# Dense expert layer of a four-layer model: rounding the weights to their high halves moves from GpSimd to ScalarE

## The reference

```python
def _L1_ffn_ref(hidden_states, Wg, Wu, Wd):      # Wg, Wu: 8 x 256 x 1024, Wd: 8 x 1024 x 256
    x = hidden_states.reshape(-1, H)
    def expert_step(acc, w):
        wg, wu, wd = w
        h = jax.nn.silu(x @ wg) * (x @ wu)
        return (acc + h @ wd, None)
    acc, _ = jax.lax.scan(expert_step, jnp.zeros_like(x), (Wg, Wu, Wd))
    return acc.reshape(B, S, H)
x = x + jnp.tanh(g_ffn[1]) * _L1_ffn_ref(_layernorm(x, axis=-1), ...)
```

## Time and profile before

| what | value |
|---|---|
| median of 3 runs | 2197.32 us (2195.87 to 2203.53) |
| profiled execution, its own time | 2206.47 us |
| its span, first to last instruction | 2204.7 us |
| mean granted TensorE clock | 0.924 |
| TensorE matmul busy | 1898.4 us (86%) |
| VectorE busy | 1589.9 us (72%) |
| ScalarE busy | 1046.2 us (47%) |
| GpSimd busy | 793.9 us (36%) |
| the dense stage | from about 516 us to 1574 us of the span |

### The profile page before, as it was taken

One profiled execution on the slowest core, in us unless ns is written; L12 is line 12 of the kernel. 1 busy time (PEld: TensorE's weight loads), 2 busy tenths in 40 slices (PEclk: granted clock), 3 DMA queues, 4 the chain that ended last, 5 costly groups with the idle time before them and its releaser, 6 DMA issues.

```text
span 2204.7 us, 31887 instructions
## 1 busy us (share of the span) xinstructions
PE 1898.4 (86%) x9854; PEld 1583.8 (72%) x9854; DVE 1589.9 (72%) x2416; ACT 1046.2 (47%) x1863; POOL 793.9 (36%) x732
## 2 busy tenths in 40 slices
PE   6669995895999999999999999999766995995894
PEld 3459995684777777777777777777646995784894
DVE  4847776668888888888888888888744665565574
ACT  4327773334444444454454444445333772332672
POOL 3012331435444444544543544543002222430341
PEclk8859998997999999999999999999976997995897
DMA  3035662000000000000000000030104433002453
GB/s 113 19 106 184 193 187 80 5 0 29 15 29 29 14 29 29 14 29 29 19 24 29 28 14 29 29 128 19 39 13 141 143 112 97 4 0 77 147 163 127
DMA packets 113555, 138.59 MB, mean 63 GB/s; under 512 B 15332, under 2 KB 101606, under 8 KB 113504
## 3 DMA queue, kind: packets, MB, share of 16 engines
q1 hardware_dynamic: 105952, 121.70, 17.5%
q0 software_dynamic: 7552, 16.24, 2.7%
HBM read 117.22 MB, written 24.90 MB: 64 GB/s over the span
## 4 chain that ended last, share of the span: by engine, by line
PE 66%; issue 13%; DVE 11%; ACT 4%; POOL 3%; DMA 2%; DVEq 0%; ACTq 0%; SPq 0%; another core or an unknown queue 0%; POOLq 0%
PE ps L644 34%; PE ps L836 10%; PE ps L837 9%; PE ps L838 9%; POOL sc L527 2%; PE ps L655 1%; POOL xs L523 1%; ACT ps L1352 1%; DVE h_act L1635 1%; ACT wsplit L1337 1%; DVE xs L1893 1%; DVE bn L1448 1%; DVE lnx L1441 1%; PE ps L985 1%; PE ps L1026 1%
## 5 line engine op out<-in xcount | busy, mean ns | idle before, releaser
L644 PE MATMUL ps<-h_hi,wsplit 128*128 128x512 f32 (+3 forms) x2016 | 603.7, 352 | 27.4 <-issue 24.9
L644 PEld LDWEIGHTS ps<-h_hi,wsplit 128*128 128x128 f32 x2016 | 366.8, 188 | 91.7 <-issue 45.0
L532 POOL TENSOR_TENSOR wsplit<-wraw,zero 128x256 fp32r<-128x256 f32 (+2 forms) x160 | 190.7, 1207 | 492.8 <-PE ps L838 363.9
L644 PE MATMUL ps<-h_lo,wsplit 128*128 128x512 f32 (+3 forms) x1008 | 352.4, 350 | 0.0
L1650 DVE TENSOR_TENSOR h_lo<-h,h_hi 128x512 fp32r<-128x512 f32 x256 | 304.1, 1209 | 44.7 <-ACT h_hi L1283 44.7
L1283 ACT ACTIVATE h_hi<-h 128x512 fp32r<-128x512 f32 x256 | 155.0, 629 | 293.2 <-DVE h L1646 153.7
L644 PE MATMUL ps<-xTh,wsplit 128*128 128x256 f32 (+2 forms) x992 | 260.0, 316 | 15.1 <-DVE h_lo L1845 8.7
L1270 ACT ACTIVATE lnx<-ps 128x512 f32<-128x512 f32 x384 | 207.4, 596 | 54.2 <-PE ps L838 54.0
L1845 DVE TENSOR_TENSOR h_lo<-ps,h_hi 128x256 fp32r<-128x256 f32 (+2 forms) x248 | 117.5, 474 | 156.4 <-ACT h_hi L1356 147.8
L1279 ACT ACTIVATE h_act<-h_act 128x512 f32<-128x512 f32 x192 | 121.3, 632 | 190.3 <-DVE h_act L1635 189.2
L836 PE MATMUL ps<-xTh,wsplit 128*128 128x512 f32 x512 | 204.0, 398 | 3.9 <-ACT lnx L1270 2.2
(11 more groups left out here) (284 smaller groups left out, 3709.1 us busy)
## 6 DMA issues: line engine op xcount, KB each, us to landing
wraw<-in_L_w SPq DMA_DIRECT2D x124, 512.0 KB, 3.4
wraw<-in_L_ffn_Wg SPq DMA_DIRECT2D x32, 256.0 KB, 2.9
wraw<-in_L_ffn_Wu SPq DMA_DIRECT2D x32, 256.0 KB, 3.3
wraw<-in_L_ffn_Wd SPq DMA_DIRECT2D x32, 256.0 KB, 3.7
x_tok<-lnx SPq DMA_DIRECT2D x12, 512.0 KB, 3.8
lnx<-y_tok SPq DMA_DIRECT2D x12, 512.0 KB, 5.9
y_tok<-lnx SPq DMA_DIRECT2D x3, 2048.0 KB, 14.0
wat<-in_attn SPq DMA_DIRECT2D x16, 256.0 KB, 5.1
```

The costliest lines, as they stand in the source:

```text
L532: return pool.tensor_tensor(out_, in_, zero[:, :].to_broadcast(shape), ALU.add)
L644: return pe.matmul(out_, lhsT, rhs, start=start, stop=stop)
```

## The change

The rounding to high halves leaves GpSimd and goes to ScalarE, as `ACT.Copy` activations. `w_up_high(u+1)` (512, 256 and 1024 columns; the two blocks of 256 are now one instruction) stands in the group with `tp = 0` and `w_down_high(u+1)` (512 columns) in the group with `tp = 1`, both between `silu("21")` and `high("21")`. GpSimd keeps the four sums and the low halves, and now waits for ScalarE's `p_whi` ahead of each low half; its waits for `p_up` and `p_down` go, and ScalarE waits for `p_up >= 14G` instead. For unit 0 the highs stand at the head of ScalarE's stage, behind the table load. The last unit prepares nothing.

```diff
             def ffn1(n):
-                def high(out_, in_, shape):
-                    return pool.tensor_tensor(out_, in_, zero[:, :].to_broadcast(shape), ALU.add)
...
-                    for k in range(KD):
-                        high(hi[:, k, :, :], raw[:, :, k, 0, :], [P, 2, P]).then_inc(p_whi, 1)
-                    high(hi[:, 2, :, :], raw[:, :, 1, 1, :], [P, 2, P]).then_inc(p_whi, 1)
                     pool.wait_ge(p_wsum, 4 * u + 3)
                     pool.tensor_tensor(w_sums[:, 3, :, :], raw[:, :, 1, 0, :], w_sums[:, 2, :, :], ALU.subtract).then_inc(p_wsum, 1)
+                    pool.wait_ge(p_whi, 4 * u + 1)
                     for k in range(KD):
-                        pool.wait_ge(p_whi, 5 * u + k + 1)
                         pool.tensor_tensor(lo[:, k, :, :], raw[:, :, k, 0, :], hi[:, k, :, :].bitcast(F32), ALU.subtract).then_inc(p_wup, 1)
-                    pool.wait_ge(p_whi, 5 * u + 3)
+                    pool.wait_ge(p_whi, 4 * u + 2)
                     pool.tensor_tensor(lo[:, 2, :, :], raw[:, :, 1, 1, :], hi[:, 2, :, :].bitcast(F32), ALU.subtract).then_inc(p_wup, 1)
-                    pool.wait_ge(p_wsum, 4 * u + 4)
-                    high(hi[:, 3:7, :, :], w_sums[:, :, :, :], [P, 4, 2, P]).then_inc(p_whi, 1)
-                    pool.wait_ge(p_whi, 5 * u + 4)
+                    pool.wait_ge(p_whi, 4 * u + 3)
                     pool.tensor_tensor(lo[:, 3:7, :, :], w_sums[:, :, :, :], hi[:, 3:7, :, :].bitcast(F32), ALU.subtract).then_inc(p_wup, 1)
-                    if not start:
-                        pool.wait_ge(p_down, 4 * (u - 1))
-                    high(d_hi, raw_down[z], [P, 2, D]).then_inc(p_whi, 1)
-                    pool.wait_ge(p_whi, 5 * u + 5)
+                    pool.wait_ge(p_whi, 4 * u + 4)
                     pool.wait_ge(p_wup, 4 * (u + 1))
                     pool.tensor_tensor(d_lo, raw_down[z], d_hi.bitcast(F32), ALU.subtract).then_inc(p_wdown, 1)
...
+                def w_up_high(u, z):
+                    act.wait_ge(p_raw[z], 24 * (u - z) + 48)
+                    raw, hi = raw_up[z], pair_up[z][0]
+                    act.activation(hi[:, 0:2, :, :].rearrange("p k m w -> p m k w"), raw[:, :, :, 0, :], ACT.Copy).then_inc(p_whi, 1)
+                    act.activation(hi[:, 2, :, :], raw[:, :, 1, 1, :], ACT.Copy).then_inc(p_whi, 1)
+                    act.wait_ge(p_wsum, 4 * (u + 1))
+                    act.activation(hi[:, 3:7, :, :], w_sums[:, :, :, :], ACT.Copy).then_inc(p_whi, 1)
+
+                def w_down_high(u, z):
+                    act.activation(pair_down[z][0], raw_down[z], ACT.Copy).then_inc(p_whi, 1)
...
                     silu(G, "21")
+                    if not end and tp == 0:
+                        if not first:
+                            act.wait_ge(p_up, 14 * G)
+                        w_up_high(u + 1, 1 - z)
+                    if not end and tp == 1:
+                        w_down_high(u + 1, 1 - z)
                     high(G, "21")
+                w_up_high(0, 0)
+                w_down_high(0, 0)
                 copy(0)
```

More of the change, by code:

```diff
@@ L530, in ffn1, with unit @@
             def ffn1(n):
-                def high(out_, in_, shape):
-                    return pool.tensor_tensor(out_, in_, zero[:, :].to_broadcast(shape), ALU.add)
-                def unit(u, z, start=False):
-                    pool.wait_ge(p_raw[z], 48 if start else 24 * (u - z) + 48)
+                def unit(u, z):
+                    pool.wait_ge(p_raw[z], 24 * (u - z) + 48)
                     raw, (hi, lo), (d_hi, d_lo) = raw_up[z], pair_up[z], pair_down[z]
@@ L540, in unit @@
                     pool.tensor_tensor(w_sums[:, 2, :, :], w_sums[:, 0, :, :], raw[:, :, 0, 0, :], ALU.subtract).then_inc(p_wsum, 1)
-                    if not start:
-                        pool.wait_ge(p_up, 28 * (u - 1))
-                    for k in range(KD):
-                        high(hi[:, k, :, :], raw[:, :, k, 0, :], [P, 2, P]).then_inc(p_whi, 1)
-                    high(hi[:, 2, :, :], raw[:, :, 1, 1, :], [P, 2, P]).then_inc(p_whi, 1)
                     pool.wait_ge(p_wsum, 4 * u + 3)
                     pool.tensor_tensor(w_sums[:, 3, :, :], raw[:, :, 1, 0, :], w_sums[:, 2, :, :], ALU.subtract).then_inc(p_wsum, 1)
+                    pool.wait_ge(p_whi, 4 * u + 1)
                     for k in range(KD):
-                        pool.wait_ge(p_whi, 5 * u + k + 1)
                         pool.tensor_tensor(lo[:, k, :, :], raw[:, :, k, 0, :], hi[:, k, :, :].bitcast(F32), ALU.subtract).then_inc(p_wup, 1)
-                    pool.wait_ge(p_whi, 5 * u + 3)
+                    pool.wait_ge(p_whi, 4 * u + 2)
                     pool.tensor_tensor(lo[:, 2, :, :], raw[:, :, 1, 1, :], hi[:, 2, :, :].bitcast(F32), ALU.subtract).then_inc(p_wup, 1)
-                    pool.wait_ge(p_wsum, 4 * u + 4)
-                    high(hi[:, 3:7, :, :], w_sums[:, :, :, :], [P, 4, 2, P]).then_inc(p_whi, 1)
-                    pool.wait_ge(p_whi, 5 * u + 4)
+                    pool.wait_ge(p_whi, 4 * u + 3)
                     pool.tensor_tensor(lo[:, 3:7, :, :], w_sums[:, :, :, :], hi[:, 3:7, :, :].bitcast(F32), ALU.subtract).then_inc(p_wup, 1)
-                    if not start:
-                        pool.wait_ge(p_down, 4 * (u - 1))
-                    high(d_hi, raw_down[z], [P, 2, D]).then_inc(p_whi, 1)
-                    pool.wait_ge(p_whi, 5 * u + 5)
+                    pool.wait_ge(p_whi, 4 * u + 4)
                     pool.wait_ge(p_wup, 4 * (u + 1))
@@ L563, in unit @@
                     pool.wait_ge(p_wdown, u + 1)
-                unit(0, 0, start=True)
+                unit(0, 0)
                 pool.wait_ge(tr_done, NG * (n + 1))
-                unit(1, 1, start=True)
+                unit(1, 1)
                 pool.wait_ge(p_xlo, 14)
@@ L1283, in high, with group @@
                     act.activation(h_hi[:, SLOT[c], :], h_32[:, c in ("12", "21"), :], ACT.Copy).then_inc(p_hi, 1)
-                def group(G, first=False, x_next=False):
+                def group(G, u, z, tp, first=False, x_next=False, end=False):
                     if not first:
@@ L1321, in ffn1 @@
                     x_high(op, 0)
[L1322 to L1325, removed]
+                group(0, 0, 0, 0, first=True, x_next=True)
+                group(1, 0, 0, 1)
+                group(2, 1, 1, 0)
+                group(3, 1, 1, 1)
+                with act.Fori(2, UNITS - 2, 2) as u:
+                    for z in range(2):
+                        for tp in range(2):
+                            group(2 * (u + z) + tp, u + z, z, tp)
+                for u in range(UNITS - 2, UNITS):
                     for tp in range(2):
-                        group(G + tp)
+                        group(2 * u + tp, u, u % 2, tp, end=u == UNITS - 1)
             def moe(layer, n):
```

## The result

| | changed | before | ratio, 95% interval |
|---|---|---|---|
| median of 4 runs | 2145.77 us (2140.55 to 2150.14) | 2199.09 us (2195.87 to 2203.53) | 0.9755 (0.9726 to 0.9784) |
| profiled execution, its own time | 2146.34 us | 2206.47 us | |
| its span | 2144.6 us | 2204.7 us | |

The changed kernel is faster by 2.45%, 53 us at the medians. The forecast was 2143 us, 2131 to 2180.

The account below looks back on a forecast made before the run. TensorE, busy 862.5 of 900 us, was taken to set the pace. 52.9 us saved by closing both gaps in the loop plus 1 us at the start made 54 us: 2197.3 - 54 = 2143 us, range 2131 to 2180.

Parts of the forecast that it names:

- Gap A: TensorE idle ahead of down `j=0`, waiting for the last low half of h; 1.01 us per unit, forecast to go.
- gap B: TensorE waiting for VectorE's g12 sum, once per unit; 0.78 us including the next too long distance, forecast to go.
- ScalarE's chain: Three roundings ahead of `high("21")`, 1.8 us of starts, hidden under the 2.67 us wait for `product("21")`.
- The race: `lower("21")`, asked for at 937.73, must precede GpSimd's boundary at 938.1, before the 1024-column low half; margin about 0.4 us.
- GpSimd's load: GpSimd loses 160 roundings, 190.7 us in all; worth nothing by itself, only when its other instructions run counts.
- The start: Start of the stage, with unit 0 prepared later, behind ScalarE's table load; -1 us, bounds -8 and +5.
- the low clock: TensorE at low clock (0.43 us between starts) in group 0, returning perhaps 2 us of the token sums' gain.
- The statistics: Statistics instructions at the start of the stage no longer meet GpSimd; about -2.5 us.
- The layer norm: Layer norm at the start of the stage now meets unit 0's low halves on GpSimd; about +5 us.
- TensorE's wait for the token sums in group 0: Preparing unit 1 collided with group 0's token sums, TensorE waiting 8.31 us; most of it to go, about -5 us.
- Group 0's tail: End of group 0 at the start of the stage meets unit 1's low halves; +1 to +3 us.
- the first rival: `lower("21")` comes too late, the 1024-column low half goes first: +1.2 us per unit, about 2207 us; chance 0.12.

Follow-up runs that it names:

- Experiments 1 and 2: Changed kernel plus one more ScalarE copy between its 1024-column rounding and `high("21")`: 256 columns in the first, 2140.68 us; 512 in the second, 2237.73 us.
- Experiments 5 and 6: First: kernel before, GpSimd's 1024-column low half waiting for `lower("11")`, 2174.47 us. Second: changed kernel, sums and low halves of units 2 to 31 cut to one column per block, 2143.97 us.
- experiment 7: Changed kernel with `high("21")` ahead of ScalarE's roundings in every group: 2141.45 us, 0.9735 of the kernel before.
- experiment 8: The changed kernel itself, measured once more on the same chip: 2141.13 us, 0.9732 of the kernel before.

## Why the prediction was right

**Gap A and gap B.** Forecast 30 x 1.01 + 29 x 0.78 = 52.9 us; the loop measured 54.5. The forecast counted the too long distance behind gap B (0.11) but not the one behind gap A, from the 940.05 of the earlier trace rows to the next start:

```profile
940.37 0.39 PE L644 MATMUL ps<-h_lo,wsplit 128*128 128x512 f32 x1
```

That is 0.32 for 0.23, or 2.7 us in 30 units, and with it 55.6. TensorE is busy 900 of 900 us where 897 was said. The unit is (976.3 - 884.0) / 3 = 30.8 us by the starts of GpSimd's 1024-column low half. The mean `lower` in the window went from 1.26 to 0.72 us.

**ScalarE's chain.** Forecast 0.63, 0.42 and 1.05 us; measured 0.62, 0.41 and 1.05, in 1.78 us from the first start to the start of `high("21")`. It didn't even wait for `product("21")` (ended 913.40). No wait of ScalarE for `p_up`, `p_raw` or `p_wsum` shows in the window.

**The race.** Forecast margin about 0.4 us; measured 0.41. Experiments 1 and 2 are the proof: +0.31 us on ScalarE costs nothing, +0.51 costs 2.13 us per unit. That a waiting VectorE instruction goes first at a boundary of two GpSimd instructions was read from a single row, and held in all 30 units of the loop: GpSimd's 1024-column low half shows between 2.858 and 2.872 us in each, and no `lower` in the loop more than 1.27. The rule of the Trainium skill ("SBUF — State Buffer", section "Who interferes with whom"), that the pair is held for a whole instruction, agrees with 2.76 against 0.69 us. What decided here is the order at the boundary, and that is shown by the rows alone.

**GpSimd's load is worth nothing by itself.** Experiments 5 and 6 show it from both sides: half of the gain at an unchanged load, and no further gain at a sixth of it.

**The start.** Forecast -1 us within -8 and +5, measured -4.2. The -1 is not the sum of its parts: -2.5 + 5 - 5 + 2 and +1 to +3 make +0.5 to +2.5, so the parts were further off than the total. The sign of each part that was named was right, but for the low clock. The rows (statistics and layer norm, then a token sum of group 0 that took 2.85 in the earlier trace rows):

```profile
504.38 0.19 DVE L1436 TENSOR_TENSOR st_sum<-bn 128x16 f32<-128x16 f32 x1
...
505.92 9.62 DVE L1452 TENSOR_SCALAR lnx<-xs,st_mean,st_rstd 128x256 f32<-128x256 f32 x16
...
526.41 0.68 DVE L1631 TENSOR_TENSOR lnx<-xT 128x512 f32<-128x512 f32 x1
...
542.19 2.86 DVE L1661 TENSOR_TENSOR h_lo<-h,h_hi 128x512 fp32r<-128x512 f32 x1 [0.70 <-ACT h_hi L1281]
```

The statistics end 2.7 us earlier (said 2.5). The layer norm takes 9.62 us against 5.25 before, +4.4 (said 5). TensorE's wait for the token sums in group 0 fell from 8.31 to 3.92 us, -4.4 (said -5). Group 0's tail lost its race: in this one group the `lower` comes behind the boundary, takes 2.86 us, and TensorE waits 2.44 (its matmuls then stand 0.43 us apart until about 549). So the first rival did occur once, at the place where the forecast had +1 to +3. The marks split it in two: TensorE's last wait for a token sum in group 0 ends 6.4 us earlier, counted from the first statistics instruction (532.90 - 504.38 against 539.06 - 504.13), and the tail gives 2.2 of that back. Of the 6.4 the named parts make 2.7 - 4.4 + 4.4 = 2.7. Two waits that the forecast had not priced make another 2.6: before, TensorE also waited 1.7 us for VectorE's low halves of the tokens and 0.9 us for an earlier sum in group 0, and neither wait is left. The last 1.1 us are TensorE's clock. Ahead of its long wait it has twelve matmuls; before, they take 5.8 us without their wait (524.08 to 530.76, less 0.92), at a granted clock of 0.51, and after 4.65 us (524.34 to 528.99), at 0.62 to 0.64. So the mis-sized terms are the token work of group 0, -5 in the forecast and -7.0 in its waits, and the low clock, +2 in the forecast and -1.1 as measured: behind the wait the slow stretch is as long as before (532.90 to 538.16 against 539.06 to 544.33). That experiment 7 wins 2.7 us at this very place fits the lost race.

**The sum.** The marks give -58.7 us, the profiled executions -60.1, the medians -53.3. The rest of 1.4 us between the first two lies outside these marks. The 7 us between the executions and the medians are the height of before's profiled execution above its median, as the forecast had taken into account. 2145.8 is 3 us above the forecast. That it is so close is partly luck: the forecast said 54 us for loop and start together, and the marks give 58.7. The changed kernel measured once more (experiment 8) is 58.2 us below the kernel before, nearer to the marks than to the 53.3 of the first result, though the two intervals overlap.

## What to carry to other kernels

Lay the timelines of the engines that share SBUF side by side, and ask of each long GpSimd instruction which VectorE instruction it meets and who waits for that one. Moving one by a single wait gave half of the gain here (28 of 54.5 us), with no work taken away. Where a short instruction has to come ahead of a long one, work out the margin in both directions, and if there is an order that needs no margin (here `high("21")` first, at the same time), take that. Gaps that are gone can't be won twice: once TensorE is busy 900 of 900 us, look elsewhere.

## What the runs showed of the hardware that was not expected

- A gap's price isn't only its length. With 2.05 us of extra idle once per unit TensorE's clock fell to 1.2 GHz for spells behind 24 of the 30 gaps (0.52 granted in one of 3.4 us, 0.96 over the loop), and that cost another 1.52 us each, 36.5 us in all. With 1.01 us once and 0.78 us once per unit it stayed at 2.4 GHz. Why one gap was followed by it and another not stays open.
- The layer norm's one-input instruction, `TENSOR_SCALAR` with SBUF data, is held up by GpSimd too: 9.62 us for 16 beside GpSimd's low halves, 5.26 without.
- At a boundary between two queued GpSimd instructions the waiting VectorE instruction went first, in 0.1 us of margin too (experiment 1).
